# Layer 2 output projection: heads 0 to 14 of four token tiles are multiplied inside the heads stage, and all its weights are loaded there

## The reference

```python
q = silu(conv(x @ Wq)); k = silu(conv(x @ Wk)) * D ** (-0.5); v = silu(conv(x @ Wv))
alpha = sigmoid(x @ Wa + ba); beta = sigmoid(x @ Wb + bb)
def step(St, inp):
    sk = einsum('bhij,bhj->bhi', St, k_)
    err = sk - v_
    Sn = a_ * St - b_ * err * k_
    o_ = einsum('bhij,bhj->bhi', Sn, q_)
    return (Sn, o_)
o = (o - mu) * rsqrt(var + 1e-05) * ln_w + ln_b      # per head
o = (o * sigmoid(x @ Wg)).reshape(B, S, NH * D)
return o @ Wo                                        # 2048 -> 256, added to x
```

## Time and profile before

| | us |
|---|---|
| median of three runs | 2323.51 (2321.5 to 2327.88) |
| the profiled execution, its own time | 2320.97 |
| its span, first to last instruction | 2319.2 |
| mean granted TensorE clock | 0.905 of full |
| last head's tail, last product issued to end of the gate | 1827.2 to 1839.2 |
| projection stage | 1840.2 to 1910.8 |

### The profile page before, as it was taken

The page is one execution under the profiler, slowest core; times in us unless marked ns, Lnnn a source line. Parts: engine busy times, 40 slices in busy tenths (PEclk is TensorE's granted clock), DMA queues, the critical chain, the costliest instruction groups (busy, mean ns, idle before and its releaser), DMA issues. The chain is left out here.

```text
span 2319.2 us, 52385 instructions
## 1 busy us (share of the span) xinstructions
PE 1939.5 (84%) x21291; PEld 1337.0 (58%) x21293; DVE 1214.6 (52%) x3220; ACT 836.5 (36%) x1973; POOL 459.6 (20%) x536
## 2 busy tenths in 40 slices
PE   7994779997999996676899999999999797779568
PEld 3542654565677664454666676666666674546445
DVE  6657542434465335734566566666666227552541
ACT  1012321221453222232666657666665202220120
POOL 0002320232000322551221122122121003710200
PEclk9997989997999997786999999999999798799679
DMA  4000000341500425752001001000100217730000
GB/s 160 0 0 14 1 5 1 121 180 47 218 1 4 128 83 167 242 195 82 30 21 40 21 21 40 21 21 24 37 21 21 65 33 238 239 134 2 9 7 19
DMA packets 55235, 157.39 MB, mean 68 GB/s; under 512 B 12803, under 2 KB 29785, under 8 KB 50726
## 3 DMA queue, kind: packets, MB, share of 16 engines
q1 hardware_dynamic: 45110, 128.84, 16.7%
q0 software_dynamic: 9888, 25.20, 3.3%
HBM read 115.36 MB, written 40.48 MB: 67 GB/s over the span
## 5 line engine op out<-in xcount | busy, mean ns | idle before, releaser
L2247 PE MATMUL l_heads_ps_p<-xnT,l2a_w 128*128 128x512 f32 x512 | 253.5, 620 | 8.6 <-DMA l2a_w<-in_l_w_heads 8.6
L2647 DVE SCALAR_TENSOR_TENSOR l_heads_taps<-l_heads_padded,l_heads_conv,l_heads_taps 128x1024 f32<-128x1024 f32 x144 | 183.7, 1286 | 8.2 <-ACT l_heads_taps L2473 7.5
L2247 PEld LDWEIGHTS l_heads_ps_p<-xnT,l2a_w 128*128 128x128 f32 x512 | 88.4, 191 | 79.9 <-issue 63.2
L206 PE MATMUL norm_turn<-zeros,ident 128*128 128x512 f32 x120 | 66.1, 707 | 53.9 <-PEq L60 53.9
L2822 POOL TENSOR_TENSOR l_heads_e<-l2a_table,l_heads_row 128x512 f32<-128x512 f32 x32 | 33.3, 1042 | 389.9 <-DVE l_heads_first L2658 384.5
L197 ACT ACT_TABLE_LOAD x10 | 12.8, 1283 | 217.9 <-PEq L60 217.9
L379 PE MATMUL l_ffn_a_ps_w<-l_ffn_a_term,ident 128*128 128x512 f32 x240 | 76.7, 473 | 8.9 <-DVE l_ffn_a_term L477 8.9
L578 POOL TENSOR_TENSOR l_qkv_by_sin<-l_qkv_raw,l_qkv_angle 128x512 f32<-128x512 f32 (+1 forms) x16 | 23.2, 1451 | 284.0 <-ACT l_qkv_raw L566 280.6
L206 PEld LDWEIGHTS norm_turn<-zeros,ident 128*128 128x128 f32 x120 | 26.1, 226 | 88.2 <-issue 88.2
L2473 ACT ACTIVATE l_heads_taps<-l_heads_ps_p,l_heads_conv 128x512 f32<-128x512 f32 x96 | 76.0, 792 | 0.0
L2472 ACT COPY l_heads_padded<-l_heads_ps_p 128x512 f32<-128x512 f32 x96 | 56.5, 589 | 52.5 <-PE l_heads_ps_p L2247 52.5
(11 more groups left out here) (697 smaller groups left out, 4924.6 us busy)
## 6 DMA issues: line engine op xcount, KB each, us to landing
l_results<-zeros SPq DMA_DIRECT2D x24, 512.0 KB, 6.2
l_ffn_a_w_in<-in_l_in_w SPq DMA_DIRECT2D x8, 1536.0 KB, 10.7
l_ffn_b_w_in<-in_l_in_w SPq DMA_DIRECT2D x8, 1536.0 KB, 9.5
l2a_w<-in_l_w_heads SPq DMA_DIRECT2D x16, 512.0 KB, 3.7
l_heads_row<-l_rows SPq DMA_DIRECT2D x16, 512.0 KB, 4.8
l_ffn_a_w_out<-in_l_out_w SPq DMA_DIRECT2D x8, 768.0 KB, 8.5
l_ffn_a_w_in<-l_results SPq DMA_DIRECT2D x8, 768.0 KB, 6.5
l_ffn_b_w_out<-in_l_out_w SPq DMA_DIRECT2D x8, 768.0 KB, 8.4
```

The costliest lines, as they stand in the source:

```text
L206: pe.matmul(turn[:, i % KC, (i // KC) % HALVES, :], core.ident[:], core.zeros[:, 0:HALF], start=True, stop=True)
L2247: mm = pe.matmul(ps_p[half][:], w[b][:, which, c, :], core.xnT[:, c, half * HALF:(half + 1) * HALF], start=(c == 0), stop=(c == KC - 1))
L2647: dve.scalar_tensor_tensor(out=taps[which][:], in0=padded[which][:, :, j:j + SEQ], scalar=conv[p % 2][:, which, j:j + 1], in1=taps[which][ ...
```

## The change

- The four weight parts now have four tiles that live through the heads stage and the projection stage. The heads stage uses them as `w[0]`, `w[1]`, `taps[0]` and `taps[1]` (q and k), and SP loads a part into each of them when its last use there is over: part 0 after the last gate projection of head 14, part 3 when the features of k of head 15 are ready, part 2 when those of q are, part 1 after the last gate projection of head 15. The projection stage loads no weights.
- Four of the recurrence's six banks (`bank01`, `bank02`, `bank10`, `bank11`) are now lent by tensors that live as long, and are the four banks of the projection.
- At the end of PE's list of the heads stage, PE waits for the four parts, for the gate of head 14 and for the last readers of the four banks. Then it multiplies heads 0 to 14 of tiles 0 and 1 (30 matmuls), does the two `turn_o` of head 15, and multiplies heads 0 to 14 of tiles 2 and 3 (30 more).
- In the projection stage PE begins with head 15 of tiles 0 to 3 (4 matmuls) and goes on as before. The order on DVE is the same.

```diff
-def wide_project_stage(nc, core, name, oT, project, early, heads, l3):
+def wide_project_stage(nc, core, name, oT, project, heads, l3):
...
         def _(sp):
-            for i in range(2):
-                project.load(sp, 2 + i, late[i])
...
-            for half in range(2):
-                some = range(half * heads // 2, (half + 1) * heads // 2)
-                for i in (2 * half, 2 * half + 1):
-                    pe.wait_ge(project.loaded[i], 16)
-                for t in range(TILES // 2):
-                    add_heads(t, some)
+            for t in range(TILES // 2):
+                project.add_heads(pe, oT, t, range(heads - 1, heads)).then_inc(projected, 1)
             pe.wait_ge(rank_loaded, 64)
...
-        taps = [st.sb(f"taps{i}", [P, BATCH, SEQ]) for i in range(3)]
+        taps = [*(wide.tiles[2 + i][:].rearrange("p (s n) -> p s n", s=BATCH) for i in range(2)),
+                st.sb("taps2", [P, BATCH, SEQ])]
...
-            for b in range(2):
-                sp.wait_ge(filled["p1"], nth["p1", "g", HEADS2 - 2 + b])
-                project.load(sp, b, w[b])
+            sp.wait_ge(filled["p1"], nth["p1", "g", HEADS2 - 2])
+            wide.load(sp, 0)
+            sp.wait_ge(feat_ready[K], HEADS2)
+            wide.load(sp, 2 + K_TAPS)
+            sp.wait_ge(feat_ready[Q], HEADS2)
+            wide.load(sp, 2 + Q_TAPS)
+            sp.wait_ge(filled["p1"], nth["p1", "g", HEADS2 - 1])
+            wide.load(sp, 1)
...
+            for i in (0, 2, 3, 1):
+                pe.wait_ge(wide.loaded[i], 16)
+            pe.wait_ge(gated, HEADS2 - 1)
+            for name, what in (("b01", "u"), ("b02", "state"), ("b10", "ks"), ("b11", "u")):
+                pe.wait_ge(read[name], nth[name, what, HEADS2 - 1])
+            for t in range(2):
+                wide.add_heads(pe, oT, t, range(HEADS2 - 1))
             turn_o(HEADS2 - 1, 0)
             turn_o(HEADS2 - 1, 1)
+            for t in range(2, TILES // 2):
+                wide.add_heads(pe, oT, t, range(HEADS2 - 1))
```

More of the change, by code:

```diff
@@ L1546, with __init__, add_heads, part @@
     PARTS = 4
-    def __init__(self, nc, weights):
-        self.weights = weights
+    def __init__(self, nc, weights, tiles):
+        self.weights, self.tiles, self.banks = weights, tiles, None
         self.per = weights.shape[0] // self.PARTS
         self.loaded = [nc.alloc_semaphore(f"wide_loaded{i}") for i in range(self.PARTS)]
-    def load(self, sp, i, at):
-        sp.dma_start(at[:].rearrange("p a c n -> p (a c n)").rearrange("p (h d) -> p h d", d=D),
-                     self.weights[i * self.per:(i + 1) * self.per].rearrange("h p d -> p h d")).then_inc(self.loaded[i], 16)
-def wide_project_stage(nc, core, name, oT, project, early, heads, l3):
+    def add_heads(self, pe, oT, t, some):
+        for h in some:
+            mm = pe.matmul(self.banks[t % 4][:, t // 4, :], oT[:, h, t * P:(t + 1) * P],
+                           self.part(h // self.per)[:, h % self.per, :], start=(h == 0), stop=(h == HEADS2 - 1))
+        return mm
+    def part(self, i):
+        return self.tiles[i][:].rearrange("p (h d) -> p h d", d=D)
+    def load(self, sp, i):
+        sp.dma_start(self.part(i), self.weights[i * self.per:(i + 1) * self.per].rearrange("h p d -> p h d")).then_inc(self.loaded[i], 16)
+def wide_project_stage(nc, core, name, oT, project, heads, l3):
     w_up, w_down, up_q, up_scale, up_a, up_b, down_q, down_scale, down_a, down_b = l3
     with Stage(nc, name) as st:
-        late = [st.sb(f"w{i}", [P, 4, KC, DH2]) for i in range(2)]
-        parts = [t[:].rearrange("p a c n -> p (a c n)").rearrange("p (h d) -> p h d", d=D) for t in (*early, *late)]
         q_up = st.sb("q_up", [P, KC, HIDDEN3], I32)
@@ L1628, in _ @@
                 pe.wait_ge(taken, t - TILES // 2 + 1)
-                add_heads(t, range(heads))
+                project.add_heads(pe, oT, t, range(heads)).then_inc(projected, 1)
                 if t == TILES // 2 + 1:
@@ L1641, in add @@
                     dve.wait_ge(projected, t + 1)
-                    dve.tensor_tensor(core.x[:, t, :], core.x[:, t, :], banks[t % 4][:, t // 4, :], ALU.add)\
+                    dve.tensor_tensor(core.x[:, t, :], core.x[:, t, :], project.banks[t % 4][:, t // 4, :], ALU.add)\
                         .then_inc(taken, 1)
@@ L2102, in l2_heads_stage @@
     with Stage(nc, "l2_heads") as st:
+        w = [wide.tiles[b][:].rearrange("p (a c n) -> p a c n", a=4, c=KC) for b in range(2)]
         conv = [st.sb(f"conv{b}", [P, 3, TAPS + 1]) for b in range(2)]
@@ L2138, in l2_heads_stage @@
         ps_p = [st.ps(f"ps_p{i}", [P, HALF]) for i in range(2)]
-        bank = [[st.ps(f"bank{c}{i}", [P, SY, P]) for i in range(3)] for c in range(2)]
+        lent = [b[:].rearrange("p t (s n) -> p (t s) n", n=P) for b in wide.banks]
+        bank = [[st.ps("bank00", [P, SY, P]), *lent[0:2]], [*lent[2:4], st.ps("bank12", [P, SY, P])]]
         tile_of_bank = {f"b{c}{i}": bank[c][i] for c in range(2) for i in range(3)}
@@ L2857, in l2_attention @@
         oT = ctx.enter_context(nc.sbuf_tensor("l2a_oT", [P, HEADS2, TOKENS], F32))
-        w = [ctx.enter_context(nc.sbuf_tensor(f"l2a_w{b}", [P, 4, KC, DH2], F32)) for b in range(2)]
-        project = WideProject(nc, w_out)
+        tiles = [ctx.enter_context(nc.sbuf_tensor(f"l2a_w{b}", [P, HEADS2 // 4 * D], F32)) for b in range(4)]
+        project = WideProject(nc, w_out, tiles)
         with nc.sbuf_tensor("l2a_table", [P, HEADS2, COLUMNS, TILES], F32) as table:
             l2_decay_stage(nc, core, w_gates, b_gates, table, rows)
-            l2_heads_stage(nc, core, w_heads, conv_heads, table, rows, ln_w, ln_b, oT, w, l3[:2], project)
-        wide_project_stage(nc, core, "l2_project", oT, project, w, HEADS2, l3)
+            project.banks = [ctx.enter_context(nc.psum_tensor(f"l2a_bank{q}", [P, 2, D], F32)) for q in range(4)]
+            l2_heads_stage(nc, core, w_heads, conv_heads, table, rows, ln_w, ln_b, oT, l3[:2], project)
+        wide_project_stage(nc, core, "l2_project", oT, project, HEADS2, l3)
 def l2_experts_stage(nc, core, name, t, xn, results, cleared, held):
```

11 lines of the change are left out of this document (2 added, 9 removed).

## The result

Twenty runs of each kernel gave a median of 2325.68 us for the changed kernel and 2320.85 us for the kernel before. One run of each (2490.86 and 3301.92 us) was far slower than the rest and is left out of the ratio. The ratio is **1.0026, with a 95% interval from 1.0013 to 1.0038**: 3 to 9 us slower. The forecast was 2.9 us faster.

The account below looks back on a forecast made before the run. PE was taken to bound the projection stage, the DMA chain running beside it. Tile 4 at -3.6 us (including barrier +3.7, transfers -1.4) and clock +0.7 gave -2.9, from 2323.5 to 2320.6 us; range 2315.5 to 2326.5.

Parts of the forecast that it names:

- What bounds the kernel now: Projection stage: PE bounds it, with 6.0 us of slack before tile 4; chains to there 33.4 us (PE) and 27.4 (DMA).
- What is moved: Out of the projection stage: 60 matmuls at 0.216 us, 13.0 us; PE's own chain about 14.8 us shorter, not usable in full.
- the rivals: Whole kernel: PE's saving counts in full (gain over 7.0 us, 0.08), clock falls (0.05), work only moved (0 to +7, 0.15).
- "clock falls" case: Tail: moved matmuls run at half clock, 25.8 us instead of 13.0, total 2334; chance 0.03 in full, 0.05 in all.
- The turns: Heads stage's tail: first 30 matmuls end at 1834.9, so the output's turn is at most 0.1 us late.
- The DMA chain: Projection stage: without two 512 KB weight loads ahead, the transfers come 1.4 us earlier after the barrier, ends 0 and -4.2.
- The clock: Tile 4 in the projection stage: starts at half clock after a 12 us standstill, costing +0.7 us, ends 0 to +1.4.
- The sum: Tail and projection stage together: -3.6 + 0.7 = -2.9 us, ends -7.0 and +2.6.
- the side to which I had given 0.15: Whole kernel: an outcome between 0 and +7 us, chance 0.15; slower by over 0.3%, chance 0.05.

Follow-up runs that it names:

- e3: Against the kernel before: weight parts loaded in the heads stage and banks lent, but no matmul moved; stretch 83.60 us, ratio 0.9989.
- e5: Kernel before with DVE's adds of tiles 0 to 3 placed ahead of its scaling; stretch 79.88 us, ratio 0.9998.
- e1: Changed kernel with only tile 0 worked ahead of the turns and tile 1 behind them (30 passes each); stretch 74.13 us, ratio 0.9981.
- e6: Changed kernel with 30 passes ahead of the turns, 30 behind, and DVE's adds first; stretch 70.74 us, ratio 0.9943 to the kernel before.
- e10: The e6 kernel once more, unchanged; stretch 70.74 us, ratio 0.9939 to the kernel before.
- e4: Changed kernel with DVE's adds of tiles 0 to 3 ahead of the scaling of w_up and w_down; stretch 74.21 us, ratio 0.9974.
- e2: Changed kernel with only tile 0 (30 passes) ahead of the turns, nothing behind them; stretch 71.36 us, ratio 0.9976 to the kernel before.
- e9: Changed kernel with 30 passes ahead of the turns, 12 behind, and DVE's adds first; stretch 70.73 us, ratio 0.9943 to the kernel before.
- e8: The kernel before once more, unchanged; stretch 83.51 us, ratio to itself 1.0010.

## Why the prediction was wrong, step by step

**What bounds the kernel now**: right. Six us of slack ahead of tile 4, DVE's wait for `s_down` right behind it, and two chains from the barrier: e3, e5 and the wait of 13.98 us in the changed kernel show it. e3 moved the transfers alone and gained nothing, e5 moved the adds alone and left tile 4 in place.

**What is moved (the failed step).** The prediction wrote "60 matmuls. At the full clock they go at 0.216 us each", 13.0 us. The 60 are the program's matmuls, read from the diff; the 0.216 us is the spacing of the trace's. The earlier trace rows has x64 in 13.98 us for tiles 0 to 3 and heads 8 to 15, which the program's list, shown with the change, has as x32. One float32 matmul of the program stands in this trace as two, so the count was 120, and 26 us were moved. The error entered twice with opposite signs, in the tail and in the stage, but not evenly: all of it is paid in the tail, where PE's hole ahead of the turns is 6.4 us long, and nothing of it is got back in the stage, where the DMA chain already bounded tile 4. By the prediction's own steps with 60 passes in each group: 1828.4 + 13.1, turns until 1842.5, 13.1 more until 1855.6, a barrier 16.4 us later. Measured: 15.9.

The same slip stands in the rivals: the "clock falls" case had the 60 passes at 0.43 us as 25.8 us, and in effect the full clock did that much.

**The turns**: the step "the turn is not late by more than 0.1 us" was wrong in the changed kernel (they came 6.3 us after the four tiles that the first of them needs) and right in e1, where the amount was the one that I had in mind. The waits ahead of the group cost nothing to be seen (1832.93 follows directly on the last product), and the clock stayed at 1.00 from 1831 to 1859.

**The DMA chain**: direction right, size wrong. Forecast -1.4 us with ends 0 and -4.2; measured -4.0 in the changed kernel and in e3. In eight of the nine traces in which that wait shows, `w_down` was scaled 20.2 to 21.2 us after the barrier without the weight loads; in e6 it was 23.5, and 20.2 when the same kernel was run again (e10), so the landing scatters too. The -1.4 doesn't quite follow from its own rows: I had put the beginning of `q_up`'s data at 1845.2, which is 5.0 us after the barrier and not 5.2, so the gain would be 1.2; and 1 MB as a fifth of the 20.5 us stream is 4.1, not 4.2. Half-us windows of the transfers before and, below them, after:

```profile
1845.50:1846.00 0.50, 1.00 1.32 131
1846.00:1846.50 0.50, 1.00 0.92 94
1846.50:1847.00 0.50, 1.00 0.74 127
1847.00:1847.50 0.50, 1.00 0.95 369
```

```profile
1864.50:1865.00 0.50, 1.00 0.26 90
1865.00:1865.50 0.50, 1.00 0.91 377
...
1880.00:1880.50 0.50, 0.50 0.70 117
```

Between the weights and the first fast stretch there are 1.5 us in which the DMA engines' busy share was 0.74 to 1.32 but only 94 to 131 GB/s were moved. Fast data began 6.8 us after the barrier before (1847.0 - 1840.17) and 4.2 us after it now (1865.0 - 1860.81), 2.6 us earlier, and the stream thinned out some 2.8 us earlier (at about 22.4 and 19.6 us). The landing gained 1.2 us more behind that. The estimate from the 358 GB/s of the Trainium skill ("DMA: Bandwidth & Descriptors", Specifications), 2.9 us for the megabyte, was nearer than mine. A slow stretch is there after as well, without the weights (72, 164 and 90 GB/s in the three half microseconds from 1863.5); that it belongs to the small operands is likely and not shown.

**The clock**: the half clock at the start of tile 4 was right, its cause and the comparison were not. The windows of PE, before, then after, then e4, which has no standstill:

```profile
1878.00:1892.00 14.00, 14.00 (x64) 0.99 0.00 0
1892.00:1898.00 6.00, 6.00 (x15) 0.50 0.00 0
1898.00:1911.00 13.00, 12.31 (x56) 0.98 0.00 0
```

```profile
1831.00:1859.00 28.00, 27.32 (x136) 1.00 0.00 1
1864.00:1865.00 1.00, 0.66 (x2) 1.00 0.63 127
1865.00:1866.00 1.00, 1.00 (x4) 0.80 1.00 393
1866.00:1871.00 5.00, 4.31 (x6) 0.50 1.04 282
1871.00:1884.00 13.00, 0.00 (x0) 0.50 0.80 172
1884.00:1888.00 4.00, 3.71 (x9) 0.50 0.02 4
1888.00:1919.00 31.00, 30.59 (x137) 0.98 0.00 0
```

```profile
1871.00:1872.00 1.00, 1.00 (x3) 0.63 1.00 406
1872.00:1878.00 6.00, 6.00 (x12) 0.50 1.05 256
1878.00:1879.00 1.00, 1.00 (x5) 0.96 1.08 346
```

After the standstill the half clock lasted 5.3 us into tile 4, 2.6 us lost against 1.7 before: +0.9, near the +0.7. But the clock hadn't fallen in the standstill. It fell at 1865.6, 1.3 us into the rank products of 16 rows, behind 5 us (1859 to 1864) of which PE was busy for 2.84; in e4 it fell at much the same place (5.2 us after the barrier, 4.8 here) and came back 3.4 us into tile 4, without a wait between them. By this comparison the standstill prolonged a half clock that was there already, by 1.9 us of tile 4, which is about 1 us of time. And before there was a second stretch, from 1891.7 to 1898.6, from 2.5 us into the second rank products on, which cost another 3.3 us. I had let it stand as common to both, and it is not there after. e2 with no half clock in this part needs 32.2 us; 37.2 and 34.7 are that plus 5.0 and plus 2.5. The Trainium skill ("TensorE: Matmul & The Clock Gate", HAM oscillation) has groups of matmuls start cold behind waits. Tile 4 did start at half clock, but the standstill ahead of it was not the origin, and by that rule alone this part should have become longer; it became shorter.

**The sum with the right count** would have been 16.4 - 1.4 - 6.0 + 0.1 + 0.7 = +9.8 us. The barrier came 0.5 us earlier, the transfers 2.6 us, and the clock term was 3.2 us lower: 9.8 - 0.5 - 2.6 - 3.2 = +3.5, the measured stretch. So that the forecast was off by 6.4 us and not by the 12.7 that the count alone makes is luck: three other terms erred the other way. The median, 2325.7 us, lay inside the range around the three runs' 2323.5 that I started from; against twenty runs of before, 2320.85, it is a loss, the side to which I had given 0.15 (up to 7 us) and 0.05 (above).

**Open**: the timed gains of e1, e2 (twice), e4 and e5 fall short of what their stretch shows by 3 to 7 us, and the changed kernel's timed losses (6.0 and 7.2 us) are larger than its 3.3 to 3.6, while e6, e9 and e10 agree with theirs within 1.4 us. For e4, e5 and the changed kernel the stretch lies inside the timed interval, for e1 and e2 outside. The heads stage, 739 to 755 us long, varies by more than this, but nothing shows that it depends on the kernel.

## What to carry to other kernels

Take the count and the duration of a step from the same list: where the program's order has x32 and the trace x64, multiply the trace's duration by the trace's count. Before work is moved into a hole, measure the hole against it: thirty passes of 6.5 us ahead of the turns were free, sixty made the turns 6.3 us late, and whatever stood behind the gate's end moved the barrier one to one (+3.7 us in e1). Then ask what was second behind the stage that is relieved: here loads, scaling and adds queued in one order on DVE took the gain. Moving one line there turned the changed kernel's 3.5 us of loss in the stretch into 9.3 of gain, while in the kernel before (e5) the same move left tile 4 in place.

## What the runs showed of the hardware

- The pattern of half and full clock behind the barrier repeated to about 0.3 us between executions in which everything ahead of it was shifted by up to 25 us: half clock from 34.5 to 38.0 and from 51.5 to 58.5 us behind the barrier in three traces (before, e8, e3), the same part taking 37.20 or 37.21 us each time; 34.74 and 34.79 in the two traces of the changed kernel; 32.20 twice. I had expected chance. Edits ahead (e5, e9) moved or removed whole dips of 3.4 or 6.9 us; the same work from tile 4 on took 32.2 us in e2 and 37.2 in the kernel before, and the 5 us between them are the clock's.
- PE under steady matmuls of 128 rows kept the full clock for 27 us (after, 1831 to 1859). Behind 17 us and more of PE busy without a gap, the clock fell to half in rank products of 16 rows in some cases (17.5 us after the barrier in e10, 51.6 in the kernel before) and not in others (both groups in e2, the second in e5 and e10).
- The heads stage, the same instructions each time, took from 739 to 755 us, with a granted clock of 0.86 to 0.91 in its first 100 us.
